# A chain of rotations as triangular products: three 64x64 products a level, level one of the next batch moved, VectorE's preparation split

## The chip, the cores and the metric

One core of a Trainium2 chip runs the whole kernel. The metric is the time on the device in microseconds (us), median of several runs. The engines are TensorE (PE, its weight loads PEld), VectorE (DVE), ScalarE (ACT), GpSimd (POOL) and SyncE (SP), which issues most DMAs.

## The reference, cut to what matters

Four graph layers, each followed by a residual and a layer norm, run over 3125 nodes of 256 features and 50000 edges. The changed part belongs to the last one. There, every edge with source i and target j is a rotation of two rows of a 256-row matrix by the edge's weight (an index past the end is clamped where it is read and dropped where it is written, so edges with both ends at 256 or above do nothing), and the rotations are applied one after another:

```python
def step(mat, t):
    i, j, theta = t
    c = jnp.cos(theta)
    s = jnp.sin(theta)
    ri = mat[i]
    rj = mat[j]
    mat = mat.at[i].set(c * ri - s * rj)
    mat = mat.at[j].set(s * ri + c * rj)
    return (mat, None)
mat, _ = jax.lax.scan(step, jnp.eye(256), (idx_i, idx_j, rots))   # src, dst, edge_weight
x = _layernorm(x + x @ mat.T)
```

## The kernel before

The phase `order_and_rotate` does three things side by side. POOL scatters records by indirect DMA: first the list of rotations (`steps`, 392 scatters), then the edges sorted by target (`sd_rec`, 392) and by source (`sb_rec`, 392), all through `scatter` (L236, L240). DVE computes the places for these, and then, from `rotation_masks` on, all engines but POOL work on the rotation matrix M (256x256). POOL is not held up by them, nor they by POOL once the list is there. The next phase, `sort_tables`, begins when all of this is done, with a load of `sd_rec` (L266).

The rotations are taken in batches of CB = 4 chunks of CS = 64 rotations; the loop runs over batches, `h` is the parity of the batch and picks one of two buffers. The size of the loop is read from the data; here it is 32 batches. A chunk of 64 rotations has 128 rows of coefficients (two rows a rotation: 64 rotations in two groups of 32, `early` in partitions 0 to 63 and `late` in 64 to 127). Its effect on M is M += S' R M, with S the selection of rows, R the product of an inverted triangular matrix (TF) with the coefficients (Bm). TF is found by doubling, HL = 5 levels for blocks of 32 rotations, and one last step that joins early and late.

For a batch b the engines do this, in the order of their queues:
- SP: `fetch`, four small DMAs of the batch's rotations.
- DVE: T from Lm and Am of level zero plus the identity (L584); then for the levels 1 to 4: `copied` (Y out of PSUM, L567), one part of the preparation of the next batch (`parameters`, `rights` which is Bm, `lefts` which is la, `levels` which is Lm), and the add T += ps_w (L601). Then TF's two diagonal blocks, `turned` (Am), and S (L608).
- PE: for each level the products of Lm and Am with T (L666), `ahead` (a product of R and M for one chunk of the batch before, L638), in level two `rows`, in level four `turn`, then, once ACT has copied the products into V, the products V x T (L677), and `applied` (S' Y added to M in PSUM, L646). After the levels the two products of the last step (L683, L688) and TF x Bm (L696).
- ACT: the copies ps_v to V (L722), ps_m to M (`kept`, L711), and at the end VX, TF's corner and R.

M of a chunk depends on M of the chunk before: `ahead`, `copied`, `applied`, `kept` are that chain, one link a level. V, Lm and Am hold 128x128 blocks with zeros outside the two diagonal blocks of 64x64, which carry the data of the levels:

```python
for c in range(CB):
    for kind, left in ((0, Am), (1, Lm)):
        mm = pe.matmul(ps_v[:, c, kind, :], left[:, h, c, v, :], T[:, c, kind, :], start=True, stop=True,
                       skip_group_check=True)
mm.then_inc(s["v"], 1)
ahead(b, v - 1)
```

Of the kernel before, what the change touches and what calls it, by code (L numbers as in the profile page):

```python
# [5 lines left out]
ALU = mybir.AluOpType  # L6
# [462 lines left out]
def rotation_masks(dve, K, B, s):  # L469

    LV = (CS - 1).bit_length()
# [4 lines left out]
    link(dve.tensor_scalar(kc[:, 2:3], kc[:, 0:1], 1, HS, ALU.logical_shift_right, ALU.bitwise_and))  # L476
    link(dve.tensor_tensor(kc[:, 1:2], kc[:, 1:2], kc[:, 2:3], ALU.bitwise_or))
    for v in range(LV):

        link(dve.tensor_scalar(ki[:, 1, :], ki[:, 0, :], CS - 1, v, ALU.bitwise_and, ALU.logical_shift_right))  # L480
# [4 lines left out]
        link(dve.tensor_scalar(kcf[:, 2:3], kcf[:, 0:1], -1.0, None, ALU.add))  # L485
        link(dve.tensor_scalar(mask[:, v, :], kf[:, :], kcf[:, 2:3], kcf[:, 1:2], ALU.is_equal, ALU.mult))
# [8 lines left out]
    link(dve.memset(B["V"][:, :, :, :].rearrange("p c k n -> p (c k n)"), 0.0))  # L495
# [6 lines left out]
    link(dve.memset(B["S"][:, :, :].rearrange("p c n -> p (c n)"), 0.0))  # L502
# [4 lines left out]
def rotation_vector(dve, K, B, s):  # L507

    LV = (CS - 1).bit_length()
    NCH = 9 + 2 * (2 * CB + 1) + 7  # L510
    mask, maskT, rc, rec2, w, own, oth, alpha, beta, la, lb = (B[n] for n in
                                                               "mask maskT rc rec2 w own oth alpha beta la lb".split())
    Lm, Am, Bm, Bx, S, T, TF, Y, ps_r, ps_a, ps_w, ps_y, batches = (B[n] for n in
                                                                    "Lm Am Bm Bx S T TF Y ps_r ps_a ps_w ps_y batches".split())
# [21 lines left out]
    def rights(link, h):  # L536
        for c in range(CB):
# [4 lines left out]
        link(dve.tensor_tensor(Bm[:, h], Bm[:, h], Bx[:, :, :], ALU.add))  # L542

    def lefts(link, b, h):
        dve.wait_ge(s["row"], b + 1)
        for c in range(CB):
            link(dve.tensor_scalar(la[:, c, :], ps_r[:, c, :], own[:, h, c:c + 1], alpha[:, c:c + 1],
                                   ALU.is_equal, ALU.mult))
# [24 lines left out]
    rights(link, 0)  # L573
    lefts(link, 0, 0)
    levels(link, 0)
    turned(link, 0, 0)
    with dve.Fori(0, n) as i:
        for h in range(2):
            b = i * 2 + h
            link = loop_linker(dve, s["chain3"], b, NCH)  # L580
            dve.wait_ge(s["r"], b + 1)
            for kind, left in ((0, Lm), (1, Am)):
                for at in (early, late):
                    ins = dve.tensor_tensor(T[at, :, kind, :], left[at, h, :, 0, at],  # L584
                                            B["eye"][at, :].unsqueeze(1).broadcast_to([CS, CB, CS]), ALU.add)
                    if kind == 0 or at == early:
                        link(ins)
            ins.then_inc(s["tt"], 1)
            for v in range(1, HL):
                copied(b, v - 1)  # L590
                if v == 1:
                    parameters(link, b + 1, 1 - h)
# [1687 lines left out]
```

## Time and profile before

| | |
|---|---|
| median of 3 runs | 7918.79 us (7906.65 to 7920.52) |
| profiled execution | 7903.8 us, span 7902.0 us |
| mean granted PE clock | 0.811 |
| PE busy, PEld busy | 4781.0 us (61%), 3939.6 us (50%) |
| DVE, ACT, POOL busy | 5336.5, 1288.0, 4441.6 us |

### The profile page before, as it was taken

The page shows a single profiled execution, that of the slowest core. Times are in us where ns is not written, and L with a number is a line of the kernel's source. Part 1 is how long each engine was busy: PE and PEld are TensorE (multiplying, and loading weights), DVE is VectorE, ACT ScalarE, POOL GpSimd, SP SyncE. Part 2 cuts the span into 40 slices and gives each one's busy share as a digit, 9 for nine tenths or more (in the row PEclk, how much of TensorE's full clock was granted, in tenths as well). Part 3 has the DMA queues.
Part 4 walks back from the last instruction along what each step waited for, and adds up shares of the span by engine and source line. Part 5 has one row for each costly group of instructions (what it writes and reads, how often), then busy time and mean ns, then how long its engine had stood idle before and what let it go on. Part 6 is the DMA issues. An engine that isn't in the chain of part 4 may idle for free. (4 is left out here: it accounts for less than half of the span.)

```text
span 7902.0 us, 174461 instructions
## 1 busy us (share of the span) xinstructions
PE 4781.0 (61%) x58063; PEld 3939.6 (50%) x58063; DVE 5336.5 (68%) x12256; ACT 1288.0 (16%) x2955; POOL 4441.6 (56%) x3974
## 2 busy tenths in 40 slices
PE   0000577777855355468888678888688787355551
PEld 0000576767743244347777567776477775233331
DVE  7999655555548455657777467775577774578878
ACT  0000111121210111112222112221122221122210
POOL 5888777771000577317777257774277770177730
PEclk9999878888875555589999899999899998655555
DMA  0000000000010444246664166661467640244420
GB/s 27 1 4 1 1 1 1 1 1 0 0 28 5 111 131 132 77 122 193 197 193 118 43 190 197 195 185 32 132 193 199 193 108 12 50 114 111 110 74 16
DMA packets 708566, 691.55 MB, mean 88 GB/s; under 512 B 234981, under 2 KB 589355, under 8 KB 708165
## 3 DMA queue, kind: packets, MB, share of 16 engines
q0 software_dynamic: 227328, 446.06, 20.8%
q1 hardware_dynamic: 480846, 240.51, 11.0%
q8 instruction: 216, 3.54, 0.2%
q14 instruction: 176, 1.44, 0.1%
HBM read 766.03 MB, written 77.58 MB: 107 GB/s over the span
## 5 line engine op out<-in xcount | busy, mean ns | idle before, releaser
L1601 POOL DMA_INDIRECT kvring<-kvtab,oth x1776 | 1984.3, 1117 | 825.4 <-issue 425.6
L1001 POOL DMA_INDIRECT e_hg<-htab,oth_d x992 | 1015.4, 1024 | 1478.0 <-issue 1420.8
L1652 PE MATMUL ea_pss<-ea_qb,ea_kT 128*128 128x128 f32 x7104 | 1018.9, 276 | 0.0
L1652 PEld LDWEIGHTS ea_pss<-ea_qb,ea_kT 128*128 128x128 f32 x7104 | 945.1, 194 | 16.1
L1722 DVE TENSOR_TENSOR acc<-ea_psg,acc 128x64 f32 x1776 | 399.3, 225 | 611.9 <-PE ea_psg L1663 538.6
L1696 ACT ACTIVATE ea_kT<-ea_pst 128x512 f32<-128x512 f32 x888 | 482.1, 595 | 2023.0 <-PE ea_pst L1640 2006.8
L1640 PE MATMUL ea_pst<-ident,kvring 128*128 128x128 f32 x3552 | 489.2, 281 | 474.7 <-DMA kvring<-kvtab,oth 473.7
L1640 PEld LDWEIGHTS ea_pst<-ident,kvring 128*128 128x128 f32 x3552 | 385.8, 142 | 553.1 <-DMA kvring<-kvtab,oth 343.4
L240 POOL DMA_INDIRECT steps<-or_rec,or_rplacei x392 | 566.9, 1446 | 135.5 <-issue 135.5
L1736 DVE TENSOR_REDUCE ea_sc<-ea_pss 128x64 f32<-128x1024 f32 x444 | 540.7, 1218 | 48.1 <-PE ea_pss L1652 48.1
L1764 DVE TENSOR_TENSOR ea_mix<-ea_hot,ea_att 128x1024 f32<-128x1024 f32 (+1 forms) x444 | 544.9, 1227 | 0.1
L1663 PE MATMUL ea_psg<-ea_mix,kvring 128*64 128x64 f32 x14208 | 519.6, 227 | 13.5 <-DVE ea_mix L1764 13.1
L1649 PE MATMUL ea_pss<-mrow,ea_mk 128*128 128x256 bf16 x1776 | 491.2, 277 | 56.6 <-ACT ea_kT L1696 24.9
L1663 PEld LDWEIGHTS ea_psg<-ea_mix,kvring 128*64 128x64 f32 x14208 | 457.9, 139 | 88.7 <-issue 85.9
L236 POOL DMA_INDIRECT sd_rec<-or_drawrec,or_dplacei x392 | 406.2, 1036 | 125.3 <-issue 123.3
L236 POOL DMA_INDIRECT sb_rec<-or_srawrec,or_splacei x392 | 395.0, 1008 | 124.3 <-issue 122.9
L1128 PEld LDWEIGHTS e_psg<-e_Em,e_hg 128*32 128x32 f32 x15872 | 320.3, 145 | 217.6 <-DVE e_Em L1221 205.1
L1128 PE MATMUL e_psg<-e_Em,e_hg 128*32 128x32 f32 x15872 | 360.3, 244 | 113.0 <-DVE e_Em L1221 112.8
L567 DVE COPY or_Y<-or_psy 128x256 f32<-128x256 f32 x132 | 56.1, 425 | 550.0 <-PE or_psy L638 550.0
L1197 DVE TENSOR_TENSOR accT<-e_psg,accT 128x96 f32 x992 | 255.0, 257 | 250.5 <-DVE accT L1197 215.7
L666 PE MATMUL or_psv<-or_T,or_Am 128*128 128x64 f32 x1024 | 240.8, 323 | 237.4 <-DVE or_T L601 164.1
L1176 DVE TENSOR_REDUCE e_mt<-e_pss 32x4 f32<-32x512 f32 (+1 forms) x248 | 235.0, 947 | 183.4 <-PE e_pss L1102 182.7
(508 smaller groups left out, 9761.1 us busy)
## 6 DMA issues: line engine op xcount, KB each, us to landing
ea_qb<-qtab SPq DMA_DIRECT2D x1776, 64.0 KB
qtab<-at_qst SPq DMA_DIRECT2D x75, 512.0 KB, 3.3
kvring<-kvtab,oth POOLq DMA_INDIRECT x1776
e_stack<-ohtab SPq DMA_DIRECT2D x744, 32.0 KB
kvtab<-at_kvst SPq DMA_DIRECT2D x75, 256.0 KB, 2.7
e_hg<-htab,oth_d POOLq DMA_INDIRECT x992
ea_mk<-mtab SPq DMA_DIRECT2D x444, 3.0 KB
htab<-Hd SPq DMA_DIRECT2D x2, 3200.0 KB, 13.4
```

What stands on the lines that cost most here:

```text
L236: pool.indirect_dma_start(out=rec, out_offset=bass.IndirectOffsetOnAxis(ap=placei[:, j:j + 1], axis=0), in_=rawrec[:, j, :], in_offset=Non ...
L240: pool.indirect_dma_start(out=rec, out_offset=bass.IndirectOffsetOnAxis(ap=placei[:, j:j + 1], axis=0), in_=rawrec[:, j, :], in_offset=Non ...
L1001: pool.indirect_dma_start(out=hg[:, b % RING, u, :], out_offset=None, in_=htab, in_offset=bass.IndirectOffsetOnAxis(ap=oth[:, b * 4 + u:b ...
L1128: pe.matmul(ps_g[e % 2][h * NBD:(h + 1) * NBD, u, k, :], lhs(k * P + h * NBD, NBD), Em[:, e % 2, u, k * 4 + h if H > 1 else 0, :], start=T ...
L1601: pool.indirect_dma_start(out=kv[:, b % R, u, :], out_offset=None, in_=kvtab, in_offset=bass.IndirectOffsetOnAxis(ap=oth[:, b * QB + u:b * ...
L1640: tr = pe.transpose(ps_t[:, u, k, :], kv[:, r, u, k * P:(k + 1) * P], K["ident"][:, :])
L1649: pe.matmul(ps_s[r % 2][:, u, :], mk[:, r, u * P:(u + 1) * P], K["mrow"][:, :], start=True, stop=False, skip_group_check=True)
L1652: mm = pe.matmul(ps_s[r % 2][:, u, k * 2 * HN:(k + 1) * 2 * HN], kT[:, r % 2, u, k, :], qb[:, r, u, :], start=False, stop=True, skip_group ...
L1663: mm = pe.matmul(ps_g[r % 2][c * DH1:(c + 1) * DH1, u, :], kv[:, r, u, D + g * DH1:D + (g + 1) * DH1], mix[:, r % 2, u, g * G:(g + 1) * G, ...
L1696: ins = act.activation(kT[:, r % 2, 2 * k:2 * k + 2], ps_t[:, 2 * k:2 * k + 2], ACT.Copy)
L1736: dve.tensor_reduce(sc[:, :, :, :].rearrange("p u g h -> p (u g h)"), ps_s[r % 2][:, :, :].rearrange("p u (q n) -> p (u q) n", n=NBS), AX. ...
L1764: dve.tensor_tensor(mix[:, r % 2], hot[:, bass.ds(b * QB, QB), :].unsqueeze(2) .broadcast_to([P, QB, G * G, NBS]), att[:, :, :, :].rearran ...
```

## The change

The products on the full array with zeros outside the diagonal blocks become products of 64x64 blocks, each on its own part of the array (partitions 0 to 63 to 0 to 63, 64 to 127 to 64 to 127). Lm goes; a level is now: X = Am T0 (`level`), then T1' X and X' T1 (`closed`), 8 and 16 small matmuls. ACT copies one X of 128x256 instead of two parts of V. T, la and S get two buffers. The product and the close of level one of batch b+1 go among the last step's products of batch b, and S is made early in a batch. DVE's `rights` and `lefts` are split into pairs of chunks, placed between the `copied` and the adds; level four's add is done in three parts that write TF directly. The last step's two products go to the banks of ps_R, 64x64. The masks are made for five levels and 64 columns. `turns` is a semaphore that nothing waits for.

```diff
--- before.py
+++ after.py
...
-    def rights(link, h):
-        for c in range(CB):
+    def rights(link, h, cs, last):
+        for c in cs:
...
-        link(dve.tensor_tensor(Bm[:, h], Bm[:, h], Bx[:, :, :], ALU.add))
-
-    def lefts(link, b, h):
...
+        if last:
+            link(dve.tensor_tensor(Bm[:, h], Bm[:, h], Bx[:, :, :], ALU.add))
+
+    def lefts(link, h, cs):
+        for c in cs:
...
-        link(dve.tensor_tensor(la[:, :, :], la[:, :, :], lb[:, :, :], ALU.add))
+
+    def joined(link, h):
+        link(dve.tensor_tensor(la[:, h], la[:, h], lb[:, :, :], ALU.add))
         dve.sem_inc(s["l"], 1)
-
-    def levels(link, h):
-        for c in range(CB):
-            ins = dve.tensor_tensor(Lm[:, h, c], la[:, c, :].unsqueeze(1).broadcast_to([P, LV, P]), mask[:, :, :], ALU.mult)
+        for at in (early, late):
+            ins = dve.tensor_tensor(T[at, h, :, 0, :], la[at, h, :, at],
+                                    mask[at, :].unsqueeze(1).broadcast_to([CS, CB, CS]), ALU.mult)
         link(ins)
 
     def turned(link, b, h):
         dve.wait_ge(s["turn"], b + 1)
-        for c in range(CB):
-            ins = dve.tensor_tensor(Am[:, h, c], ps_a[:, c, :].unsqueeze(1).broadcast_to([P, LV, P]), maskT[:, :, :], ALU.mult)
+        link(dve.tensor_tensor(T[:, h, :, 1, :], ps_a[:, :, :],
+                               maskT[:, 0, :].unsqueeze(1).broadcast_to([P, CB, CS]), ALU.mult))
+        link(dve.tensor_tensor(T[:, h].rearrange("p c k n -> p (c k) n"), T[:, h].rearrange("p c k n -> p (c k) n"),
+                               B["eye"][:, :].unsqueeze(1).broadcast_to([P, 2 * CB, CS]), ALU.add))
+        for v in range(1, HL):
+            ins = dve.tensor_tensor(Am[:, v - 1], ps_a[:, :, :],
+                                    maskT[:, v, :].unsqueeze(1).broadcast_to([P, CB, CS]), ALU.mult)
         link(ins)
+        dve.sem_inc(s["ti"], 1)
+
+    def added(b, h, v):
+        dve.wait_ge(s["w"], b * HL + v)
+        dve.tensor_tensor(T[:, h], ps_w[:, :, :, :], T[:, h], ALU.add).then_inc(s["tt"], 1)
...
     with dve.Fori(0, n) as i:
         for h in range(2):
             b = i * 2 + h
+            g = 1 - h
             link = loop_linker(dve, s["chain3"], b, NCH)
+            parameters(link, b + 1, g)
+            copied(b, 0)
+            dve.tensor_tensor(S[:, h], K["row"][:, :].unsqueeze(1).broadcast_to([P, CB, D]),
+                              own[:, h, :].unsqueeze(2).broadcast_to([P, CB, D]), ALU.is_equal).then_inc(s["S"], 1)
+            dve.wait_ge(s["tt"], b * 3 + 1)
+            added(b, h, 2)
             dve.wait_ge(s["r"], b + 1)
-            for kind, left in ((0, Lm), (1, Am)):
-                for at in (early, late):
-                    ins = dve.tensor_tensor(T[at, :, kind, :], left[at, h, :, 0, at],
-                                            B["eye"][at, :].unsqueeze(1).broadcast_to([CS, CB, CS]), ALU.add)
-                    if kind == 0 or at == early:
-                        link(ins)
-            ins.then_inc(s["tt"], 1)
-            for v in range(1, HL):
-                copied(b, v - 1)
-                if v == 1:
-                    parameters(link, b + 1, 1 - h)
-                if v == 2:
-                    rights(link, 1 - h)
-                if v == 3:
-                    lefts(link, b + 1, 1 - h)
-                if v == 4:
-                    levels(link, 1 - h)
-                dve.wait_ge(s["w"], b * HL + v)
-                dve.wait_ge(s["tt"], b * HL + v)
-                dve.tensor_tensor(T[:, :, :, :], ps_w[:, :, :, :], T[:, :, :, :], ALU.add).then_inc(s["tt"], 1)
-            dve.wait_ge(s["tt"], b * HL + HL)
-            link(dve.tensor_copy(TF[early, :, early], T[early, :, 1, :]))
-            link(dve.tensor_copy(TF[late, :, late], T[late, :, 1, :]))
-            dve.sem_inc(s["tz"], 1)
-            turned(link, b + 1, 1 - h)
-            dve.wait_ge(s["m"], b * CB + CB)
-            dve.tensor_tensor(S[:, :, :], K["row"][:, :].unsqueeze(1).broadcast_to([P, CB, D]),
-                              own[:, h, :].unsqueeze(2).broadcast_to([P, CB, D]), ALU.is_equal).then_inc(s["S"], 1)
+            dve.wait_ge(s["row"], b + 2)
+            lefts(link, g, (0, 1))
+            copied(b, 1)
+            lefts(link, g, (2, 3))
+            dve.wait_ge(s["tt"], b * 3 + 2)
+            added(b, h, 3)
+            joined(link, g)
+            copied(b, 2)
+            rights(link, g, (0, 1), False)
+            dve.wait_ge(s["tt"], b * 3 + 3)
+            dve.wait_ge(s["w"], b * HL + 4)
+            dve.tensor_tensor(TF[late, :, late], ps_w[late, :, 1, :], T[late, h, :, 1, :], ALU.add).then_inc(s["tl"], 1)
+            dve.tensor_tensor(T[early, h, :, 0, :], ps_w[early, :, 0, :], T[early, h, :, 0, :], ALU.add).then_inc(s["te"], 1)
+            dve.tensor_tensor(TF[early, :, early], ps_w[early, :, 1, :], T[early, h, :, 1, :], ALU.add).then_inc(s["tz"], 1)
+            turned(link, b + 1, g)
+            copied(b, 3)
+            rights(link, g, (2, 3), False)
+            added(b + 1, g, 1)
+            rights(link, g, (), True)
...
-    def turn(b):
+    def turn(b, h):
         pe.wait_ge(s["l"], b + 1)
+        pe.sem_inc(s["turns"], 1)
         for c in range(CB):
-            tr = pe.transpose(ps_a[:, c, :], la[:, c, :], K["ident"][:, :])
-        tr.then_inc(s["turn"], 1)
+            for at in (early, late):
+                mm = pe.matmul(ps_a[at, c, :], la[at, h, c, at], K["ident"][at, at], start=True, stop=True,
+                               skip_group_check=True)
+        mm.then_inc(s["turn"], 1)
+
+    def level(h, v):
+        pe.sem_inc(s["turns"], 1)
+        for c in range(CB):
+            for at in (early, late):
+                mm = pe.matmul(ps_v[at, c, :], Am[at, v - 1, c, :], T[at, h, c, 0, :], start=True, stop=True,
+                               skip_group_check=True)
+        mm.then_inc(s["v"], 1)
+
+    def closed(h):
+        pe.sem_inc(s["turns"], 1)
+        for c in range(CB):
+            for at in (early, late):
+                pe.matmul(ps_w[at, c, 0, :], T[at, h, c, 1, :], X[at, c, :], start=True, stop=True, skip_group_check=True)
+        for c in range(CB):
+            for at in (early, late):
+                mm = pe.matmul(ps_w[at, c, 1, :], X[at, c, :], T[at, h, c, 1, :], start=True, stop=True,
+                               skip_group_check=True)
+        mm.then_inc(s["w"], 1)
...
     with pe.Fori(0, n) as i:
         for h in range(2):
             b = i * 2 + h
-            for v in range(1, HL):
-                pe.wait_ge(s["tt"], b * HL + v)
-                for c in range(CB):
-                    for kind, left in ((0, Am), (1, Lm)):
-                        mm = pe.matmul(ps_v[:, c, kind, :], left[:, h, c, v, :], T[:, c, kind, :], start=True, stop=True,
-                                       skip_group_check=True)
-                mm.then_inc(s["v"], 1)
-                ahead(b, v - 1)
+            g = 1 - h
+            for v in range(2, HL):
+                pe.wait_ge(s["tt"], b * 3 + v - 1)
+                level(h, v)
                 if v == 2:
-                    rows(b + 1, 1 - h)
-                if v == 4:
-                    turn(b + 1)
+                    rows(b + 1, g)
+                ahead(b, v - 2)
                 pe.wait_ge(s["vs"], b * HL + v)
-                for c in range(CB):
-                    for kind in range(2):
-                        mm = pe.matmul(ps_w[:, c, kind, :], V[:, c, 1 - kind, :], T[:, c, kind, :], start=True, stop=True,
-                                       skip_group_check=True)
-                mm.then_inc(s["w"], 1)
-                applied(b, v - 1)
-            pe.wait_ge(s["tt"], b * HL + HL)
+                closed(h)
+                applied(b, g, v - 2)
+            turn(b + 1, g)
+            pe.wait_ge(s["tl"], b + 1)
+            pe.sem_inc(s["turns"], 1)
             for c in range(CB):
-                mm = pe.matmul(ps_v[:, c, 1, :], Lm[:, h, c, HL, :], T[:, c, 1, :], start=True, stop=True,
-                               skip_group_check=True)
+                mm = pe.matmul(ps_R[0][early, c // 2, c % 2, 0:CS], la[late, h, c, early], TF[late, c, late],
+                               start=True, stop=True, skip_group_check=True)
             mm.then_inc(s["v"], 1)
+            ahead(b, CB - 1)
+            pe.wait_ge(s["ti"], b + 2)
+            level(g, 1)
+            pe.wait_ge(s["te"], b + 1)
             pe.wait_ge(s["vs"], b * HL + HL)
+            pe.sem_inc(s["turns"], 1)
             for c in range(CB):
-                mm = pe.matmul(ps_w[0:CS, c, 1, :], T[:, c, 0, :], VX[:, c, :], start=True, stop=True,
-                               skip_group_check=True)
+                mm = pe.matmul(ps_R[1][early, c // 2, c % 2, 0:CS], T[early, h, c, 0, :], VX[early, c, :],
+                               start=True, stop=True, skip_group_check=True)
             mm.then_inc(s["w"], 1)
-            pe.wait_ge(s["rs"], b + 1)
             pe.wait_ge(s["tz"], b + 1)
+            pe.wait_ge(s["vs"], b * HL + HL + 1)
+            closed(g)
+            applied(b, g, CB - 1)
             pe.wait_ge(s["tx"], b + 1)
...
+    def product(b, v):
+        act.wait_ge(s["v"], b * HL + v)
+        act.activation(X[:, :, :], ps_v[:, :, :], ACT.Copy).then_inc(s["vs"], 1)
...
     with act.Fori(0, n) as i:
         for h in range(2):
             b = i * 2 + h
-            for v in range(1, HL):
-                act.wait_ge(s["v"], b * HL + v)
-                for at in (early, late):
-                    ins = act.activation(V[at, :, :, at], ps_v[at, :, :, :], ACT.Copy)
-                ins.then_inc(s["vs"], 1)
-                kept(b, v - 1)
+            for v in range(2, HL):
+                product(b, v)
+                kept(b, v - 2)
             act.wait_ge(s["v"], b * HL + HL)
-            act.activation(VX[:, :, :], ps_v[:, :, 1, :], ACT.Copy).then_inc(s["vs"], 1)
+            act.activation(VX[early, :, :], ps_R[0][early, :, :, 0:CS].rearrange("p a b n -> p (a b) n"),
+                           ACT.Copy).then_inc(s["vs"], 1)
+            product(b + 1, 1)
             act.wait_ge(s["w"], b * HL + HL)
-            act.activation(TF[early, :, late], ps_w[early, :, 1, :], ACT.Copy).then_inc(s["tx"], 1)
+            act.activation(TF[early, :, late], ps_R[1][early, :, :, 0:CS].rearrange("p a b n -> p (a b) n"),
+                           ACT.Copy).then_inc(s["tx"], 1)
+            kept(b, CB - 1)
             act.wait_ge(s["r"], b + 2)
             for q in range(2):
                 ins = act.activation(R[:, 2 * q:2 * q + 2], ps_R[q][:, :, :, :], ACT.Copy)
...
-            beta=sb("beta", [P, CB]), la=sb("la", [P, CB, P]), lb=sb("lb", [P, CB, P]), Lm=sb("Lm", [P, 2, CB, LV, P]),
-            Am=sb("Am", [P, 2, CB, LV, P]), Bm=sb("Bm", [P, 2, CB, D]), Bx=sb("Bx", [P, CB, D]), S=sb("S", [P, CB, D]),
-            T=sb("T", [P, CB, 2, CS]), TF=sb("TF", [P, CB, P]), V=sb("V", [P, CB, 2, P]), VX=sb("VX", [P, CB, CS]), eye=sb("eye", [P, CS]), R=sb("R", [P, CB, 2, P]), Y=sb("Y", [P, D]),
-            ps_m=pb("psm", [P, 2, D]), ps_r=pb("psr", [P, CB, P]), ps_a=pb("psa", [P, CB, P]),
-            ps_v=pb("psv", [P, CB, 2, CS]), ps_w=pb("psw", [P, CB, 2, CS]), ps_R=[pb(f"psR{i}", [P, 2, 2, P]) for i in range(2)],
+            beta=sb("beta", [P, CB]), la=sb("la", [P, 2, CB, P]), lb=sb("lb", [P, CB, P]),
```

## Rows read from the trace of the kernel before

**Rows 1.** The page: busy share of PE and its granted clock, 40 slices.
```profile
PE   0000577777855355468888678888688787355551
...
PEclk9999878888875555589999899999899998655555
```

**Rows 2.** Windows: us; PE, PEld, DVE, ACT, POOL busy; PEclk, DMA share, GB/s.
```profile
1600.00:1800.00 200.00, 155.11 (x912) 138.10 (x912) 114.63 (x223) 40.17 (x72) 152.65 (x152) 0.82 0.03 1
1800.00:2000.00 200.00, 158.54 (x920) 141.95 (x919) 111.52 (x228) 40.49 (x72) 4.97 (x5) 0.81 0.01 0
```

**Rows 3.** The tile sb_rec: POOL's scatters (min/median/max ns, first and last start), landing.
```profile
L236 POOL DMA_INDIRECT sb_rec<-or_srawrec,or_splacei x392: 953/958/1882, 1288.6 to 1805.5; - x196
...
DMA to landing us min/median/max: 2.1/2.1/3.0
```

**Rows 4.** The tile sd_rec: its first reader in the next phase.
```profile
L266 SPq DMA_DIRECT2D sd_recs<-sd_rec x1: 352/352/352, 2311.1 to 2311.1; - x1
```

**Rows 5.** Line 584, ns and first and last start: the first T products.
```profile
L584 DVE TENSOR_TENSOR or_T<-or_Lm,or_eye x64: 408/422/467, 851.9 to 2250.3; 64x256 f32<-64x256 f32 x64
```

**Rows 6.** Timeline of the loop's end: start, length, operation, idle before.
```profile
2295.77 1.08 ACT L731 ACTIVATE or_R<-or_psR 128x512 f32<-128x512 f32 x2 [3.61 <-PE or_psR L696]
...
2310.25 0.60 ACT L711 ACTIVATE M<-or_psm 128x512 f32<-128x512 f32 x1 [2.87 <-PE or_psm L646]
```

**Rows 7.** Windows of one batch, columns as in rows 2.
```profile
1983.60:2028.20 44.60, 37.13 (x200) 32.71 (x199) 25.02 (x50) 8.96 (x16) 0.00 (x0) 0.75 0.01 0
...
2002.00:2014.50 12.50, 12.11 (x47) 10.30 (x47) 4.99 (x11) 2.96 (x5) 0.00 (x0) 0.52 0.00 0
```

**Rows 8.** Timeline of that batch.
```profile
1985.57 2.02 PE L638 MATMUL or_psy<-M,or_R 128*128 128x256 f32 x4
...
1988.08 0.17 DVE L520 TENSOR_TENSOR or_w<-or_rec 128x4 f32<-128x4 f32 x1
...
1989.87 0.22 DVE L531 SCALAR_TENSOR_TENSOR or_beta<-or_rec,or_rc,or_w 128x4 f32<-128x4 f32 x1
...
1991.26 0.43 PE L666 MATMUL or_psv<-or_T,or_Am 128*128 128x64 f32 x2 [0.35 <-DVE or_T L601]
1991.48 0.30 PEld L666 LDWEIGHTS or_psv<-or_T,or_Lm 128*128 128x128 f32 x2
...
1993.10 1.08 PE L638 MATMUL or_psy<-M,or_R 128*128 128x256 f32 x4
...
2000.31 0.43 PE L666 MATMUL or_psv<-or_T,or_Am 128*128 128x64 f32 x2 [2.58 <-DVE or_T L601]
```

**Rows 9.** Timeline of that batch, line 688.
```profile
2021.52 0.68 PE L688 MATMUL or_psw<-or_VX,or_T 128*64 128x64 f32 x8 [0.47 <-ACT or_VX L726]
```

**Rows 10.** Timeline of PE in the attention stage.
```profile
4000.20 0.38 PE L1640 MATMUL ea_pst<-ident,kvring 128*128 128x128 f32 x2
4000.51 1.15 PE L1663 MATMUL ea_psg<-ea_mix,kvring 128*64 128x64 f32 x32
4001.76 0.28 PE L1649 MATMUL ea_pss<-mrow,ea_mk 128*128 128x256 bf16 x1
```

**Rows 11.** The page, group of line 1663: busy, mean ns of one.
```profile
L1663 PE MATMUL ea_psg<-ea_mix,kvring 128*64 128x64 f32 x14208 | 519.6, 227 | 13.5 <-DVE ea_mix L1764 13.1
```

**Rows 12.** DVE's groups in that batch by shape: busy, mean ns.
```profile
L556 DVE TENSOR_TENSOR or_Lm<-or_la,or_mask 128x768 f32<-128x768 f32 x4 | 3.6, 952 | 0.0
...
L542 DVE TENSOR_TENSOR or_Bm<-or_Bm,or_Bx 128x1024 f32<-128x1024 f32 x1 | 1.2, 1226 | 0.0
...
L584 DVE TENSOR_TENSOR or_T<-or_Lm,or_eye 64x256 f32<-64x256 f32 x2 | 0.8, 420 | 0.8 <-PE or_psR L696 0.8
```

**Rows 13.** Windows of the segment and the attention stage.
```profile
2460.00:2900.00 440.00, 191.08 (x4020) 135.94 (x4018) 237.84 (x619) 59.69 (x165) 215.80 (x219) 0.53 0.37 91
...
4000.00:4100.00 100.00, 82.18 (x1075) 73.12 (x1074) 73.38 (x198) 22.33 (x54) 78.35 (x72) 0.98 0.68 192
```

**Rows 14.** Timeline of POOL ahead of the loop.
```profile
785.96 1.56 POOL L236 DMA_INDIRECT sd_rec<-or_drawrec,or_dplacei  x1 [0.31 <-issue]
```

More of the change, by code:

```diff
@@ L475, in rotation_masks @@
     link(dve.tensor_scalar(kc[:, 1:2], kc[:, 0:1], HS - 1, None, ALU.bitwise_and))
[L476 to L480, printed above, removed]
+    for v in range(HL):
+        link(dve.tensor_scalar(ki[:, 1, :], ki[:, 0, :], HS - 1, v, ALU.bitwise_and, ALU.logical_shift_right))
         link(dve.tensor_copy(kf[:, :], ki[:, 1, :]))
@@ L501, in rotation_masks @@
     link(dve.memset(B["R"][:, :, :, :].rearrange("p c q n -> p (c q n)"), 0.0))
[L502 removed]
+    link(dve.memset(B["S"][:, 1].rearrange("p c n -> p (c n)"), 0.0))
     dve.sem_inc(s["S"], 1)
@@ L572, in rotation_vector @@
     parameters(link, 0, 0)
-    rights(link, 0)
-    lefts(link, 0, 0)
-    levels(link, 0)
+    dve.wait_ge(s["row"], 1)
+    lefts(link, 0, range(CB))
+    joined(link, 0)
     turned(link, 0, 0)
+    rights(link, 0, range(CB), True)
+    added(0, 0, 1)
     with dve.Fori(0, n) as i:
@@ L614, in rotation_tensor @@
 def rotation_tensor(pe, K, B, s):
-    own, la, Lm, Am, Bm, S, T, TF, V, VX, R, Y = (B[n] for n in "own la Lm Am Bm S T TF V VX R Y".split())
+    own, la, Am, Bm, S, T, TF, X, VX, R, Y = (B[n] for n in "own la Am Bm S T TF X VX R Y".split())
     ps_m, ps_r, ps_a, ps_v, ps_w, ps_R, ps_y, M, batches = (B[n] for n in
                                                             "ps_m ps_r ps_a ps_v ps_w ps_R ps_y M batches".split())
+    early, late = slice(0, CS), slice(CS, 2 * CS)
     def rows(b, h):
@@ L639, in ahead, with applied @@
         mm.then_inc(s["y"], 1)
-    def applied(k, c):
+    def applied(k, g, c):
         if c == 0:
@@ L645, in applied @@
         for q in range(2):
-            mm = pe.matmul(ps_m[:, q, :], S[:, c, q * P:(q + 1) * P], Y[:, :], start=False, stop=True,
+            mm = pe.matmul(ps_m[:, q, :], S[:, g, c, q * P:(q + 1) * P], Y[:, :], start=False, stop=True,
                            skip_group_check=True)
@@ L657, in rotation_tensor @@
     rows(0, 0)
-    turn(0)
+    turn(0, 0)
+    pe.wait_ge(s["ti"], 1)
+    level(0, 1)
+    pe.wait_ge(s["vs"], 1)
+    closed(0)
     with pe.Fori(0, n) as i:
@@ L700, in rotation_tensor @@
         ahead(n * 2, c)
-        applied(n * 2, c)
+        applied(n * 2, 1, c)
 def rotation_scalar(act, K, B, s):
-    V, VX, TF, R, ps_m, ps_v, ps_w, ps_R, M, batches = (B[n] for n in "V VX TF R ps_m ps_v ps_w ps_R M batches".split())
+    X, VX, TF, R, ps_m, ps_v, ps_R, M, batches = (B[n] for n in "X VX TF R ps_m ps_v ps_R M batches".split())
     early, late = slice(0, CS), slice(CS, 2 * CS)
+    def product(b, v):
+        act.wait_ge(s["v"], b * HL + v)
+        act.activation(X[:, :, :], ps_v[:, :, :], ACT.Copy).then_inc(s["vs"], 1)
     def kept(k, c):
@@ L715, in rotation_scalar @@
     act.sem_inc(s["rs"], 1)
+    product(0, 1)
     with act.Fori(0, n) as i:
@@ L771, in pb @@
             return ctx.enter_context(nc.psum_tensor(f"or_{name}", shape, F32))
-        full, LV = [P, RT], (CS - 1).bit_length()
+        full = [P, RT]
         B = dict(
@@ L798, in order_and_rotate @@
                 ps_o=B["ps_R"][i][:, :, :, :].rearrange("p a b c -> p (a b c)"),
-                ps_n=B[("ps_v", "ps_w")[i]][:, :, :, :].rearrange("p a b c -> p (a b c)")))
+                ps_n=(B["ps_w"][:, :, :, :].rearrange("p a b c -> p (a b c)") if i else
+                      B["ps_v"][:, :, :].rearrange("p a c -> p (a c)"))))
         names = "chain chain2 chain3 chain4 S sin sins mm pads padst placed nb init listed iota"
-        names += " rec free par row l turn v vs w tt tx tz r rs y ys m ms"
+        names += " rec free par row l turn v vs w tt ti tl te tx tz turns r rs y ys m ms"
         each = "chain cnt offs pads padst here run put tiles tilest placed row"
```

28 lines of the change are left out of this document (14 added, 14 removed).

## The prediction

> **What bounds the kernel now.** I read the slices of the page first. The rotation loop fills slices five to twelve, with PE at seven to eight tenths and its clock at 0.8; the other layers start behind it, and the change touches nothing else [rows 1]. The chain of waits on the page reaches back over the last stage alone, so the loop has to be read by windows. In the windows of 200 us the loop looks the same on both sides of 1800 us: TensorE (PE) some 157 us busy, VectorE (DVE) some 113, ScalarE 40, at a granted clock of 0.81. What differs is GpSimd (POOL): 152.7 us busy before 1800 and 5.0 after [rows 2]. The rows of POOL's own tiles say why: the last of its 784 scatters for the two sorts starts at 1805.5 us, and the next phase reads their result at 2311.1 [rows 3, 4]. So two chains run side by side in this phase. The loop ends last and sets the phase's end now; POOL's chain ends at 1805.5 + 0.96 + 2.1 for the landing = 1808.6, and the next phase would start 0.2 behind it. So as long as POOL keeps its pace, no change to the loop can give more than 2311.1 - 1808.8 = 502 us.
>
> The loop: the first T of a batch is made at 851.9, that of the last batch at 2250.3, so 31 periods of 45.1 us [rows 5]. The last batch ends at 2295.4 and the tail of four applications at 2310.85, 15.5 us later [rows 6].
>
> Within a period, PE is busy 37.1 of 44.6 us and DVE 25.0, at clock 0.75 [rows 7]. The timeline shows an alternation. In the fast stretch (granted 1.0, the level of 2.4 GHz) PE waits for DVE: level three starts at 2000.31 after 2.6 us without work, since the whole of `rights`, 5 us on DVE, stands ahead of the add of level two [rows 8]. In the slow stretch (from 2002 on granted 0.52, nearly all at the level of 1.2 GHz) PE is busy 12.1 of 12.5 us and is the bound, for its work takes almost twice as long: four wide instructions 2.02 us instead of 1.08 [rows 7, 8].
>
> **The change, PE.** A full f32 matmul of 64 columns is two instructions and comes every 0.22 us at the high level (1991.26 to 1991.48), so 0.11 for an instruction; by the ratio of the wide ones, 2.02 / 1.08 = 1.87, it is 0.21 at the low level [rows 8]. The trace has no 64x64 tile. Nearest are two. L688 has 64 weight columns and always the same part of the array: eight in 0.68 us, less some 0.23 for the last, over seven: 0.064, and 0.058 as half of the full one's pitch and a little [rows 9]. L1663 has 64 weight columns and alternates between the two column halves: 32 in 1.15 us, less 0.22, over 31: 0.030 [rows 10, 11]. So neighbours in different parts of the array overlap. The new pairs lie on the diagonal (`early`, `late`), and I take 0.030 (0.053 at the low level); the bound is L688's, no overlap, 0.058 (0.107).
>
> New PE work in a batch: levels 4 x 16, closings 4 x 32 and the turn 16 are 208 paired instructions; the two last products 16 unpaired; `rows` 8 and the product with Bm 16 full ones; `ahead` and `applied` 32 of 256 columns. At the low level: 208 x 0.053 = 11.0, 16 x 0.107 = 1.7, 24 x 0.21 = 5.1, and eight groups of four wide ones at 1.7 (their 2.02 less the end of the last one, which the next group covers) = 13.7; in all 31.5. Groups of small and full tiles now alternate, eight visits to small tiles a batch. From L1640's last start (4000.30) to L1663's first (4000.51) is 0.21 where the pitch is 0.11, and from L1663's last start (4001.44) to L1649 is 0.32 [rows 10]: about 0.3 us a visit, 8 x 0.3 = 2.4. Sum 34.0 us at the low level, about 19 at the high one. The same sum for the old batch, 160 full instructions, 4 transposes and 8 of L688, is 49.0 at the low level (33.6 + 0.8 + 0.9 + 13.7).
>
> The Trainium skill (TensorEngine Tiling (Array Packing), Key Properties) says that changing the tiling mode drains the engine, which speaks against alternating sizes; it gives no price, and the trace agrees with 0.1 to 0.2 us a change [rows 10]. The skill's TensorE: Matmul & The Clock Gate (Wait — 56ns, not 53.3ns?) says that with one way of decoding the sequencer spends about 62 ns on each matmul; by that the 208 would take 12.9 us instead of 6.2 at the high level. L1663's 0.030 speaks against it here.
>
> **The change, DVE.** Of 25.0 us busy go: Lm 3.6 and Am, of the same shape, 3.6 (L556, L562), the two Ts, four of 64x256, 1.7 (L584), the two copies into TF 0.6, one of the four adds of 128x512 0.7 = 10.2. There come: T from la, 2 x 0.42 (the 64x256 form of L584); in `turned` five of 128x256 at 0.42 (L584's length a partition) and one of 128x512 at 0.69 (a third of the way from 0.42 to L542's 1.23) = 2.8; level four in three parts of 64x256, 1.3; in all 4.9 [rows 7, 12]. That is 19.7, and 46 instructions, each some 0.04 behind the one before, add 1.8: 21.5. `lefts`, `rights`, S, `parameters` and `copied` are only moved. DVE's waits: the join of Bm and `parameters` take 1.23 + 2.0 (1988.08 to 1990.09) and the product with Bm some 1.8 beside them, so DVE is through some 1.6 us behind that product [rows 8, 12]. ScalarE's copy to R (1.08) is done by then [rows 6]. PE can do `rows` (0.9, eight at 0.11) and `ahead` (1.08), so the first Y can be copied at 3.6: a wait of 2.0. A few tenths ahead of the add of level one and at the other Ys make 0.9, an estimate from the order of the queues. Period at the high level: 24.4, with DVE as the bound; PE waits some 5 us in it. At the low level PE's 34.0 hides all of DVE, so the period is 34.0.
>
> **ScalarE.** V's copy, two of 64x512, becomes one of 128x256; it lies under `ahead` (2.02 or 1.08), as before, so nothing. If `ahead` did not cover it, each level would show some 0.4, by what DVE takes for this length. SP still fetches four pieces a batch, long ahead: nothing. The masks before the loop lose some 6 us, and the first batch's level one goes ahead of the loop, some 3 us: I take zero.
>
> **The sum.** With a share f of time at the high level, the period is 1 / (f / 24.4 + (1 - f) / 34.0). At the clock of now, 0.80 (f = 0.6): 27.5 us. Loop and tail would end at 851.9 + 32 x 27.5 + 15.5 = 1747, before POOL. POOL then sets the end: the period may be up to (1808.6 - 15.5 - 851.9) / 32 = 29.4 us, which is a granted clock of 0.70. The profiled execution took 7903.8 us (span 7902.0): 7903.8 - 502 = 7402. The median of the runs shown is 15 us above that one, so I forecast 7417, rounded to 7420.
>
> **Rivals.**
> A, the clock falls. DVE's preparation no longer fills long waits and PE has less work in the fast stretch, so less holds the clock. The segment stage, with 128x32 tiles, runs at 0.53 with PE busy 43%, the attention stage at 0.98 with 82% [rows 13]. For 0.65 the period is 30.4 and the end 1840: 7433 (7448 as a median). For 0.50 throughout, 34.0, end 1955.4: 7548 (7563). Against it: in the slow stretch PE has no waits, as in the slow stretches now, and these end by themselves.
> B, the diagonal pairs do not overlap. PE's sum is 45.2 at the low level (208 x 0.107 instead of 0.053) and some 28 at the high. At 0.80: 33.0, end 1923, 7516 (7531); at 0.65: 38.2, 7683 (7698). For it: the trace shows overlap of column halves only.
> C, POOL is slowed. Its scatters take 0.958 in the median and up to 1.88 [rows 3], and 0.30 lies between two; 392 of them in 516.9 us is one every 1.32 instead of 1.26. Ahead of the loop, under DVE's dense work in SBUF, each took 1.56 [rows 14]. So far 21 batches fell under POOL's chain, now 32: 784 x 0.06 = 47 us of slowing would become 70, +23 (7440); were every one at 1.56 + 0.30 from 851.9 on, 714 x 0.54 = 386 us, 7803. Against the latter: Lm, the longest SBUF work in the loop, is gone. From this also comes the lower bound, POOL without slowing: 7420 - 40.
> D, slower than before. B's missing overlap with the clock at its low level for the whole loop: 32 x 45.2, 7906.5 (7921), and a dearer switch decides. Above 0.35 us a visit it is over 0.2% slower; at 0.5 the loop grows by another 8 x 0.2 x 32 = 51 us and the median is 7972. It needs a clock that never rises although PE never waits.
>
> **How the numbers follow.** 0.50 for the forecast (POOL ends last), 0.30 for A, 0.12 for B, 0.05 for C, 0.03 for D. A reaches to 7563, B at today's clock to 7531; I take the range to 7600, which leaves out B at a low clock, C's extreme and D. Below, 7385. The measurement can tell some 0.2% (16 us) from no change; all but D and the worst of B are far beyond it: faster 0.96, same 0.01, slower 0.03.
>
> **What the profile of the changed kernel would show.** The next phase's read of sd_rec at some 1809 us right behind POOL's last scatter; windows with POOL busy to the end of the loop; the first T product every 25 to 29 us; a level's 16 matmul instructions in 0.7 us at the high level and 1.1 at the low; DVE some 20 us busy a batch; in fast stretches PE waiting for T and Am, in slow ones nobody ahead of PE. The forecast is wrong if the level's instructions come 0.058 apart (B), if the clock row of the loop is below 0.70 (A), or if L236's mean rises (C).

## The result and the profile after

The changed kernel takes 7416.65 us (7414.68 to 7424.07, four runs) and the one before 7917.26 us beside it: a ratio of 0.937, 95% interval 0.936 to 0.939, 500.6 us less. The forecast was 7420.

The profile was taken of a run of 7424.1 us (span 7422.3, mean granted clock 0.817). Its page shows PE, POOL and the clock in 40 slices, here of 186 us:

```profile
PE   0000488870625554788887788877788875355541
...
POOL 5888777775047760577770577760777750477720
PEclk9999999995555556999998999998999997555555
```

The loop fills slices five to nine at a clock of nine tenths, where it took eight slices of 198 us at some eight tenths [rows 1]. Windows of 200 us; PE, PEld, DVE, ACT, POOL busy, granted clock, DMA share, GB/s:

```profile
1200.00:1400.00 200.00, 166.27 (x2231) 135.03 (x2230) 155.47 (x368) 44.64 (x95) 151.77 (x151) 0.95 0.03 1
...
1600.00:1800.00 200.00, 51.99 (x606) 40.26 (x604) 41.33 (x97) 15.16 (x31) 151.11 (x156) 0.66 0.02 1
```

Now DVE is busy three quarters of the time where it was some 57% [rows 2], and the engines of the loop are through inside the second window while POOL goes on. ACT's copy to R comes twice a batch, once a half; its first and last start give the period, and the tiles sb_rec and sd_rec the end of the phase:

```profile
L771 ACT ACTIVATE or_R<-or_psR x64: 592/595/597, 874.1 to 1651.9; 128x512 f32<-128x512 f32 x64
```
```profile
L236 POOL DMA_INDIRECT sb_rec<-or_srawrec,or_splacei x392: 952/958/1880, 1290.7 to 1803.1; - x196
```
```profile
L266 SPq DMA_DIRECT2D sd_recs<-sd_rec x1: 353/353/353, 1810.3 to 1810.3; - x1
```

A batch takes (1651.9 - 874.1 - 0.5) / 31 = 25.1 us; the same copy before ran from 900.4 to 2296.3, 45.0 us a batch. The loop's engines have been idle for 145.7 us when the next phase begins; one row says so, DVE's first in it:

```profile
1803.12 0.95 POOL L236 DMA_INDIRECT sb_rec<-or_srawrec,or_splacei  x1 [0.30 <-issue]
1810.29 0.35 SPq L266 DMA_DIRECT2D sd_recs<-sd_rec  x1
1810.33 0.26 DVE L292 TENSOR_SCALAR quads<-trow_d 1x124 int32<-1x124 int32 x1 [145.69 <-PEq L55]
```

The reader is not to take the releaser literally here: PE had long been done, and the last to come was POOL. So 20 us less a batch, some 640 us in all, brought 500.8 at the phase's end (2311.1 to 1810.3). The rest is time in which PE, DVE and ACT wait for POOL's scatters. Behind the phase the engines do the same work as before, but the profiled run took 21 us longer there than the one before (7422.3 - 1810.3 = 5612.0 against 7902.0 - 2311.1 = 5590.9); the profile of e11_after_again, the same kernel run again, took 5593.3. Single runs differ by that much.

Part of the timeline of one batch, 1402.70 to 1427.80:

```profile
1403.50 1.16 PE L631 MATMUL or_psr<-ident,or_own 128*128 128x128 f32 x8 [0.21 <-DVEq L530]
...
1404.50 1.03 PE L668 MATMUL or_psy<-M,or_R 128*128 128x256 f32 x4
...
1405.57 0.42 DVE L574 COPY or_Y<-or_psy 128x256 f32<-128x256 f32 x1 [2.27 <-PE or_psy L668]
...
1407.87 0.68 PE L648 MATMUL or_psv<-or_T,or_Am 64*64 64x64 f32 x16 [0.20 <-DVE or_T L570]
...
1408.48 1.13 PE L668 MATMUL or_psy<-M,or_R 128*128 128x256 f32 x4
...
1409.54 0.68 PE L656 MATMUL or_psw<-or_X,or_T 64*64 64x64 f32 x16
...
1417.78 0.65 PE L710 MATMUL or_psR<-or_TF,or_la 64*64 64x64 f32 x8 [0.50 <-DVE or_TF L609]
...
1421.12 0.88 PE L648 MATMUL or_psv<-or_T,or_Am 64*64 64x64 f32 x16 [1.64 <-DVEq L566]
...
1422.57 1.11 PE L656 MATMUL or_psw<-or_X,or_T 64*64 64x64 f32 x16
...
1423.44 1.09 PE L659 MATMUL or_psw<-or_T,or_X 64*64 64x64 f32 x16
...
1424.57 0.69 DVE L570 TENSOR_TENSOR or_T<-or_psw,or_T 128x512 f32<-128x512 f32 x1 [1.16 <-PE or_psw L659]
```

The 16 instructions of a level come in 0.68 us; less 0.22 for the last one, they start (0.68 - 0.22) / 15 = 0.031 apart. The eight of L710 all use one part of the array and start (0.65 - 0.22) / 7 = 0.061 apart. PE's longest wait is for Am (1.64 us), and right behind it comes a stretch at the lower level: L656 has started 16 instructions when L659 begins, 0.87 / 16 = 0.054 each. Windows of that batch, before, in and behind the slow stretch:

```profile
1405.00:1421.10 16.10, 12.75 (x179) 9.46 (x178) 13.72 (x30) 2.94 (x6) 12.13 (x14) 1.00 0.03 1
1421.10:1427.40 6.30, 6.28 (x76) 6.05 (x76) 4.76 (x11) 1.36 (x3) 4.91 (x5) 0.73 0.02 1
1427.40:1440.00 12.60, 10.79 (x152) 8.30 (x152) 8.97 (x23) 3.32 (x7) 9.53 (x9) 1.00 0.04 1
```

In the slow stretch PE works 6.28 of 6.30 us and is the bound; in the fast one DVE works 13.7 of 16.1. That is the alternation of the kernel before, but the slow stretch is now a quarter of the batch or less.

### The profile page after: what moved, and what is told of

Same layout as the page of the kernel before. It is cut to its first block and busy times, and to the rows that moved or that the text cites. A ratio compares the mean times of both kernels' runs of the same rounds, so it can differ in the third digit from the quotient of the medians.

```text
span 7422.3 us, 179386 instructions
## 1 busy us (share of the span) xinstructions
PE 4338.4 (58%) x60555; PEld 3487.0 (47%) x60555; DVE 5142.6 (69%) x12108; ACT 1183.3 (16%) x2828; POOL 4449.9 (60%) x3974
## 5 line engine op out<-in xcount | busy, mean ns | idle before, releaser
L1125 PE MATMUL e_pst<-identb,e_hg 128*3 128x128 bf16 (+1 forms) x992 | 148.3, 304 | 294.4 <-DMA e_hg<-htab,oth_d 294.0
L1521 POOL MEMSET acc<- 128x12800 f32 x3 | 32.3, 10764 | 434.8 <-issue 259.5
```

## The experiments

The theory: POOL's chain ends the phase after the change, and under it the loop shortens by PE's smaller work (overlapping pairs), DVE's smaller work and the closer order. Rivals: the exit of the phase lies elsewhere; POOL is slowed; one part of the change brings nearly all. To see the loop at all, some kernels have fewer scatters for sb_rec, 272 instead of 392 ("fewer"), so that POOL is through before the loop. They leave out the last 120 columns of records, so the layers that use the source order get fewer edges; their instructions stay. Their loops are compared with e1_after_fewer.

**POOL out of the way, after and before.** Both kernels with this edit:

```diff
-    for j in range(RT):
+    for j in range(columns):
...
-                    scatter(pool, q["rec"], q["placei"], q["rawrec"], pair)
+                    scatter(pool, q["rec"], q["placei"], q["rawrec"], pair, columns=272 if q["tag"] == "s" else RT)
```

> The changed kernel with 272 instead of 392 scatters into sb_rec: the last 120 columns of records are left out, so the graph layers that use the source order get fewer edges; all their instructions stay. Theory (POOL's chain sets the end of the phase): POOL would end at 1806 - 120 x 1.31 = 1649, the loop ends at 1667 and takes over, and the next phase starts at 1668 instead of 1810: 142 us less, 7275. Rival (something else than POOL holds the phase's end): same time, 7417.

> The kernel before with the same 120 scatters left out. Theory (there the loop ends last, POOL is hidden 500 us deep): same time within 0.2%, 7917. Rival (the scatters hold the loop back, through DVE or memory): up to 120 x 0.06 = 7 us less by the slowing alone, or 142 less if POOL were on the path there too.

Measured: the changed kernel 7257.9 us, ratio 0.917 (0.915 to 0.919), 159 less than with all scatters. The kernel before: 7903.8, ratio 0.998 (0.997 to 0.999), 16 us or 0.2% less. The tiles of e1_after_fewer:

```profile
L266 SPq DMA_DIRECT2D sd_recs<-sd_rec x1: 353/353/353, 1668.4 to 1668.4; - x1
```
```profile
L236 POOL DMA_INDIRECT sb_rec<-or_srawrec,or_splacei x272: 954/958/1879, 1290.9 to 1650.3; - x136
```

The next phase now begins 0.3 us behind the loop's last copy of M (1667.54 + 0.60), 141.9 us earlier than with all scatters, and the period is the same 25.1. So POOL sets the end after the change, and the loop did before. Where the other 17 us, and the 16 us of the kernel before, come from is open. The profiles do not show it: from the next phase to the end the kernel before takes 5590.9 us and the one with fewer scatters 5590.6 (7917.7 - 2327.1), the changed kernel 5612.0 and 5593.3 and e1_after_fewer 5573.7.

**Pairs that do not alternate.** In all small products the halves go one after the other, once with fewer and once with all scatters:

```diff
-        for c in range(CB):
-            for at in (early, late):
+        for at in (early, late):
+            for c in range(CB):
```

> The kernel of the first run, with the small matmuls of a group in another order: all of the early half, then all of the late half, so that neighbours use the same part of the array. Same work. Theory (neighbours on the two diagonal tiles overlap): the spacing goes from 0.030 to 0.058 us, PE's work per batch grows by 208 x 0.028 = 5.8 us, of which DVE's waits pass on about half: period 25.1 to about 28, loop 96 us longer, 7371. Rival one (DVE alone is the bound): under 0.5 us a batch, 7290 or less. Rival two (the order makes no difference to the array): same spacing, same time, 7275.

> The changed kernel with all its scatters and the same order of the small matmuls by halves. Theory (POOL hides the loop up to a period of 29.4): the loop is some 3 us a batch longer in the trace, the time is the same within 0.2%, 7417. Rival (the loop counts all the same): 7417 + 96 = 7513.

Measured: with fewer scatters 7313.3 us (0.924), 55 above e1_after_fewer, period 26.8; with all 7411.1 (0.936), no slower than the changed kernel, period 27.1. A level of e3_halves_fewer at the high level:

```profile
1418.51 0.96 PE L648 MATMUL or_psv<-or_T,or_Am 64*64 64x64 f32 x16
```

(0.96 - 0.22) / 15 = 0.049 us on average instead of 0.031, where 0.058 was expected. The single starts in the trace are 0.058 to 0.059 apart within a half, and only where the late half begins do the two halves overlap. So neighbours on different parts of the array overlap, and those on one part do not. The cost of 1.7 us a batch is over half of the 2.9 expected; DVE is the bound for most of the batch. And what the loop loses under POOL's chain costs nothing: two us a batch, 64 in all, and the time did not move.

**Level one back behind the batch.** Level one of the next batch again behind the last products and the R product; its copy on ACT and its add on DVE move along (fewer scatters, PE's part shown):

```diff
-            pe.wait_ge(s["ti"], b + 2)
-            level(g, 1)
...
-            pe.wait_ge(s["vs"], b * HL + HL + 1)
-            closed(g)
...
+            pe.wait_ge(s["ti"], b + 2)
+            level(g, 1)
+            pe.wait_ge(s["vs"], b * HL + HL + 1)
+            closed(g)
```

> The kernel with 272 scatters into sb_rec, and level one of the next batch put back behind the product with Bm (on PE, its copy on ACT behind R's, its add on DVE behind the join of Bm). Same work. Theory (the last step's waits were filled by level one, and DVE's queue goes round without a gap): its product, copy, closing and add, some 0.7 + 0.4 + 1.1 + 0.7 = 2.9 us, come into the open between the product with Bm and level two, less the 1 us that PE waits there now: +2 us a batch, +64, 7339. Rival (DVE is the bound whatever the order on PE): 7275.

Measured: 7383.3 us (0.932), 125 above e1_after_fewer; period 29.0, 3.9 more, twice the forecast. The timeline shows why: with nothing between them, the links of level one each stand open, while PE still waits for Y.

```profile
1303.30 1.59 PE L676 MATMUL or_psm<-or_Y,or_S 128*128 128x256 f32 x4 [1.62 <-DVE or_Y L574]
...
1309.37 0.68 PE L656 MATMUL or_psw<-or_X,or_T 64*64 64x64 f32 x16 [0.93 <-ACT or_X L745]
...
1311.39 0.72 PE L648 MATMUL or_psv<-or_T,or_Am 64*64 64x64 f32 x16 [0.88 <-DVE or_T L570]
```

**DVE's preparation whole.** `lefts` and `rights` in one piece each, where their first pairs stood (fewer scatters):

```diff
-            lefts(link, g, (0, 1))
+            lefts(link, g, range(CB))
...
-            rights(link, g, (0, 1), False)
+            rights(link, g, range(CB), True)
```

> The kernel with 272 scatters into sb_rec, with DVE's preparation in whole pieces: all of lefts ahead of the second copy of Y, all of rights (with its join) ahead of level four's add. Same work. Theory (DVE is busy 19.5 of 25.1 us, with some 3 us of waits, so it is its sum that counts): the pieces delay an add by 1.8 and by 3 us, PE waits there, but DVE makes up for half of it later: +1 to +2 us a batch, 7307 to 7339. Rival (the division is what takes the waits out): +4 or more, 7400 and up. Other rival: nothing, 7275.

Measured: 7362.3 us (0.929), 104 above e1_after_fewer; period 28.3, 3.2 more with the same work on every engine, between the theory's 2 and the rival's 4. PE waits for TF once a batch:

```profile
1318.78 0.99 PE L707 MATMUL or_psR<-or_TF,or_la 64*64 64x64 f32 x8 [3.43 <-DVE or_TF L608]
1319.69 2.07 PE L665 MATMUL or_psy<-M,or_R 128*128 128x256 f32 x4
```

Behind the wait a wide group takes 2.07 us: the lower level. The division of the preparation takes waits out, and with them slow stretches.

**Small tiles alone.** The kernel before, all scatters, with its level products in 64x64 blocks and nothing else (the products of Am and Lm shown, those of V likewise):

```diff
-                        mm = pe.matmul(ps_v[:, c, kind, :], left[:, h, c, v, :], T[:, c, kind, :], start=True, stop=True,
-                                       skip_group_check=True)
+                        for at in (early, late):
+                            mm = pe.matmul(ps_v[at, c, kind, :], left[at, h, c, v, at], T[at, c, kind, :], start=True, stop=True,
+                                           skip_group_check=True)
```

> The kernel before with one part of the change alone: its four products a level, of Am, Lm and V, done as 64x64 tiles in diagonal pairs, in place; DVE, ACT and the order of all else as before. Theory: PE's work falls from 1.79 to 32 x 0.030 = 0.96 for each of eight groups, 6.6 us a batch at the high level and twice that at the low one, less 8 changes of tile size at 0.3 = 2.4; part of it lies under DVE's waits: period 45.1 to about 40, 7917 - 160 = 7757. Rival (the clock falls as PE has less work, as I feared in case A): granted clock 0.65 or less and no gain, 7900. Other rival (the tiles are the whole of the change's gain): 25 to 30 us, limited by POOL, 7417.

Measured: 7824.6 us, ratio 0.987 (0.984 to 0.991), 102 less than the kernel before beside it; period 42.3, 2.7 less. Its PE works 139.5 us in 200 where it worked 156.8, a batch 29.5 instead of 35.3, and only half of that arrives. Waits of PE from 1200 to 1400 us (total, times, longest), first of the kernel before, then of e7_tiles_only:

```profile
PE or_psv L666 <- DVE or_T L601: 22.2, 13, 3.0
```
```profile
PE or_psv L669 <- DVE or_T L601: 38.5, 15, 3.6
```

With DVE as it was, a shorter PE waits for it, and the period is 42.3 instead of the expected 40. The clock stayed at 0.79, far from the rival's 0.65.

**More work on DVE.** Three more comparisons of the shape of S a batch, 3.7 us, into a tile that nobody reads (fewer scatters):

```diff
+            for z in range(3):
+                link(dve.tensor_tensor(B["Z"][:, z], K["row"][:, :].unsqueeze(1).broadcast_to([P, CB, D]),
+                                       own[:, h, :].unsqueeze(2).broadcast_to([P, CB, D]), ALU.is_equal))
```

> The kernel with 272 scatters into sb_rec and three more instructions of S's shape (1.22 us each, into a tile that nobody reads) behind S in each batch: 3.7 us of DVE's work, about what Lm took in the kernel before. Theory (DVE's queue is the bound of the loop at the high level, and the work that went with Lm is a part of the gain): +3.2 to +3.7 us a batch, 7258 + 102 to 118 = 7360 to 7376. Rival (PE's chain through the levels is the bound, DVE's waits take the work up): +1.5 or less, 7306 or less.

Measured: 7425.2 us (0.939), 167 above e1_after_fewer; period 30.5, 5.4 more for 3.7 us of work. Where the three stand, PE waits, and then runs at the lower level:

```profile
1315.69 1.12 PE L651 MATMUL or_psv<-or_T,or_Am 64*64 64x64 f32 x16 [4.17 <-DVE or_T L570]
1316.74 2.07 PE L671 MATMUL or_psy<-M,or_R 128*128 128x256 f32 x4
```

The period takes all of DVE's added work, as the theory had it, and 1.7 us more, which neither theory nor rival had; a part of that goes with a clock of 0.86 instead of 0.95 (below).

**POOL's chain shortened.** If POOL sets the end, part of the scatters for sb_rec can go behind the loop, for nobody reads sb_rec before the tables of the second sort. The first kernel does 304 in the loop's phase, 40 beside the first sort's tables and 48 beside `type_counts`, which comes ahead of the second sort's tables; the second kernel 288, 40 and 64.

```diff
+LATER = (304, 344)
...
+            if rest:
+                @block.gpsimd
+                def _(pool):
+                    scatter(pool, *rest, K["marks"][0:2], first=LATER[0], end=LATER[1])
...
+            @block.gpsimd
+            def _(pool):
+                scatter(pool, *rest, K["marks"][0:2], first=LATER[1])
```

> The changed kernel, whole computation, with POOL's chain cut in three: 304 of the 392 scatters into sb_rec in the phase of the loop, 40 under the tables of sd, 48 under the type counts, which now come before the tables of sb. Theory (POOL is the bound of this phase and idle in the next two): POOL ends at 1806 - 88 x 1.31 = 1691, 115 us less; 40 x 1.27 = 51 us in the first table phase (some 49 long: +2) and 48 x 1.27 to 1.87 = 61 to 90 in the counts (some 70 long: 0 to +20): 7417 - 95 to - 113, about 7315. Rival (under DVE's dense work in the counts each scatter slows by more than half, as ahead of the loop): 7350 or more.

> The kernel with POOL's chain cut in three, whole computation, now 288, 40 and 64 scatters. In the run with 304, 40 and 48 the first of the three ended with the phase at 1702, 35 us behind the loop's own end, and the last one 35 us before the counts were done. Theory: the loop's phase ends 16 x 1.3 = 21 us earlier and the counts still end last (64 x 2.0 = 128 us beside their 130): 7315 - 21 = 7294. Rival (the counts' phase is stretched as much as is won): 7315.

> The changed kernel itself, beside the two others on the same chip: 7417.

Measured: 7315.3 us (0.923), then 7298.8 (0.922, interval 0.921 to 0.923); the changed kernel unaltered, on the chip of the latter, 7410.5 (0.937). So the second beats the changed kernel by 112 us and the one before by 617. Its next phase starts at 1678.1:

```profile
1678.12 0.35 SPq L272 DMA_DIRECT2D sd_recs<-sd_rec  x1
```
```profile
L237 POOL DMA_INDIRECT sb_rec<-srawrec,splacei x392: 952/958/1885, 1289.9 to 1848.1; - x196
```
```profile
1480.00:1660.00 180.00, 137.15 (x136) 0.94 0.03 1
1680.00:1840.00 160.00, 120.01 (x99) 0.50 0.15 29
```

The last fence gives windows of the tile sb_rec alone (POOL busy, clock, DMA share, GB/s): behind the loop a scatter comes every 160 / 99 = 1.62 us where it was 1.32, so moving costs something, but the last of them starts only 45 us later than in the changed kernel while the phase starts 132 us earlier.

## Why the prediction was right, step by step

**The cap.** The forecast had the phase end with POOL, at 1808.8, and 502 us of gain. It ended at 1810.3, 500.8 less; the medians differ by 500.6. One part inside was off: from the last scatter's start to the next phase it took 7.2 us (in the repeat too: 1806.6 to 1813.8), where 0.96 + 2.1 + 0.2 = 3.3 were counted. A last scatter that came 2.4 us earlier (1803.1 instead of 1805.5) hides 2.4 of these 3.9 us. What fills the 7.2 us the rows do not show. That medians, phase and forecast agree within 4 us is partly luck: the four runs of the changed kernel spread over 9 us, and the forecast for the profiled execution was 7402 where it took 7424.1.

**PE's price for an instruction of a pair.** Forecast 0.030 us at the high level and 0.053 at the low one; measured 0.031 and 0.054. The bound of no overlap, 0.058, is rival B. It is what L710 shows, all on one part (0.061), and the order by halves within a half; so the alternation is what brings 0.031. The Trainium skill's TensorE: Matmul & The Clock Gate (Wait — 56ns, not 53.3ns?) gives 62 ns a matmul for one way of decoding; at 0.031 us an instruction the trace does not show it here.

**The switch of tile size.** Forecast 0.3 us for small tiles and the way back. From the start of a level (1407.87) over a wide group (1408.48) to the closing (1409.54) pass 1.67 us. Without a switch it would be 16 x 0.031 = 0.50 for the level, and 0.92 for the wide group, as from 1993.10 to this row in the kernel before:

```profile
1994.02 1.05 PE L623 MATMUL or_psr<-ident,or_own 128*128 128x128 f32 x8
```

So the two changes of size cost 0.25 us together, nearly as counted. The Trainium skill's TensorEngine Tiling (Array Packing) (Key Properties) has a change of mode drain the engine; the trace agrees in that a change costs something, at 0.12 us each.

**PE's sum.** Forecast about 19 us at the high level. From one S to the next, without a slow stretch:

```profile
1431.15:1455.74 24.59, 19.96 (x286) 16.10 (x284) 19.27 (x47) 5.65 (x12) 17.82 (x18) 1.00 0.03 1
```

PE is busy 20.0 us in it, one more than counted, and that is still below the 24.4 of DVE's side. The 34.0 for a batch at the low level was not put to the test, as no batch ran at that level throughout.

**DVE's sum.** Forecast 19.7 busy, 1.8 between instructions, 2.0 ahead of the first Y, 0.9 of other waits, 24.4. Measured 19.5 (155.5 / 200 x 25.1), the first Y 2.27 late, the add of level one 1.16 and the other Ys 0.3 each. The periods without a slow stretch, as the one shown, are 24.2 to 24.8 long, nine of them in the loop: the 24.4 holds.

**The clock.** This assumption failed, and on the harmless side: 0.80 was taken over, and it rose to 0.95. By the forecast's own formula with f = 0.9, 1 / (0.9 / 24.4 + 0.1 / 34.0) = 25.1 us, which is the measured period. With POOL at the end the 2.4 us a batch between 27.5 and 25.1 are worth nothing, so the time came out all the same; without POOL they are 77 us. Rival A, that the clock falls, is wrong, and its reason too: PE has less work a batch, but the batch shrank more, so its busy share rose, from 553 to 585 of 700 us, and it was granted more.

**Rivals.** B fell by the 0.031. Its price was too high as well: by its own terms PE's sum at the high level is 19 + 208 x 0.028 = 24.8 and not some 28, which at 0.80 makes 30.3 us a batch and 7429, and not 7516. C fell by POOL's pace: 151.8 us busy with 151 scatters in 200, as before [rows 2], the mean of sb_rec 995 ns against 1008. D needed B and a low clock and had neither.

**Where the 20 us a batch come from.** Taken back alone, the order of pairs costs 1.7, level one's place 3.9, the division of the preparation 3.2; the small tiles alone bring 2.7 of the 19.9 from the side of the kernel before. What was not tried alone is the removal of Lm with its product and of 5.5 us of DVE work (25.0 less 19.5), nor S made early, nor level four's add in three parts, so their shares stay open. The parts act on each other, since each is worth more when the other engine is quick, so these are no shares of a sum.

## What to carry to other kernels

Before a loop is costed, ask what runs beside it: the cap of 502 us came from one row of POOL's tile and was worth more than every price in the loop, and once the loop is below it, the next gain lies in moving POOL's work (112 us here for a shift of 104 scatters). Two engines that alternate as the bound have to be shortened together and interleaved finely: small tiles alone brought half of the PE time that they saved. Give neighbouring matmuls different parts of the array: here they then start 0.031 us apart instead of 0.058.

## What was not expected of the hardware

PE was granted more clock with less work a batch. The runs compared, busy time and clock from 900 to 1600 us, and the longest wait of PE from 1200 to 1400:

| kernel | PE busy of 700 us | longest wait, us | granted clock |
|---|---|---|---|
| after | 585 | 1.6 | 0.95 |
| halves in turn | 629 | 1.6 | 0.92 |
| level one back | 545 | 1.6 | 0.91 |
| preparation whole | 569 | 3.5 | 0.86 |
| more on DVE | 536 | 4.2 | 0.86 |
| small tiles alone | 491 | 3.6 | 0.79 |
| before | 553 | 3.0 | 0.80 |

The busy time does not order them (569 has 0.86 and 545 has 0.91). The longest wait parts them in two, 1.6 us with 0.91 and more, 3.0 and more with 0.86 and less, but inside the two it does not order them either. In the timelines shown above (of the changed kernel, level one back, the whole preparation, more on DVE) a slow stretch begins right behind a wait of 1.6 to 4.2 us. But such a wait is not enough: in the changed kernel the 1.64 us come in every batch, and here no slow stretch follows:

```profile
1446.16 0.68 PE L648 MATMUL or_psv<-or_T,or_Am 64*64 64x64 f32 x16 [1.64 <-DVEq L566]
```
```profile
1440.00:1465.00 25.00, 20.37 (x302) 16.52 (x299) 19.66 (x48) 5.66 (x12) 18.29 (x19) 1.00 0.03 1
```

That the waits are the cause is argued, not shown; no run changed them alone. By the forecast's formula the clock's part is the smaller one: for the whole preparation 0.86 gives 1 / (0.72 / 24.4 + 0.28 / 34.0) = 26.5 us, 1.4 of the 3.2 more, and 1.8 stay open; for more work on DVE, 24.4 + 3.7 = 28.1 for the fast stretch gives 28.6 us at 0.95 and 29.5 at 0.86, so the clock has 0.9 of the 5.4, and 1.0 stays open.
